# Splitting the statistics and the read of g into halves of a group in a fused hypergraph block

## The reference

```
def hypergraph_conv(x, adj, W, b):
    H = (adj != 0);  w = adj.reshape(N, -1)[:, :C]
    xw = einsum('ncd,hd->nch', x, W)
    Dn = 1 / einsum('nce,ne->nc', H, w)      # 0 where the sum is not positive
    Be = 1 / H.sum(axis=1)
    m = Be[:, :, None] * einsum('nce,nch->neh', H, xw)
    return Dn[:, :, None] * einsum('nce,neh->nch', H, m) + b

h = relu(hypergraph_conv(x, adj, W1, b1))    # 256 -> 512 features
h = layer_norm(h, gamma, beta)
y = hypergraph_conv(h, adj, W2, b2) + x      # 512 -> 256 features
out = layernorm(x + y)                       # over the 256 features, no gain or shift
```

## Time and profile before

| | us |
|---|---|
| median of 3 runs (302.49 to 303.74) | 303.43 |
| the profiled execution | 302.48 |
| its span, from first to last instruction | 300.6 |
| TensorE matmuls busy | 285.8 (95%) |
| TensorE weight loads busy | 253.5 (84%) |
| ScalarE busy | 212.6 (71%) |
| VectorE busy | 208.4 (69%) |
| GpSimd busy | 126.6 (42%) |

### The profile page before, as it was taken

One profiled execution on the slowest core, in us unless ns is written; L12 is line 12 of the kernel. 1 busy time (PEld: TensorE's weight loads), 2 busy tenths in 40 slices (PEclk: granted clock), 3 DMA queues, 4 the chain that ended last, 5 costly groups with the idle time before them and its releaser, 6 DMA issues.

```text
span 300.6 us, 5790 instructions
## 1 busy us (share of the span) xinstructions
PE 285.8 (95%) x1866; PEld 253.5 (84%) x1866; DVE 208.4 (69%) x587; ACT 212.6 (71%) x621; POOL 126.6 (42%) x163
## 2 busy tenths in 40 slices
PE   7799999999999999999999999999999999999991
PEld 6689879798988979898897989889797988979790
DVE  2788496785758577585858758594866859385784
ACT  3497869688585968858596886859688685755514
POOL 2236162707245270714527171543617063362462
PEclk9999999999999999999999999999999999999998
DMA  7920500505133050603315060311405210020104
GB/s 223 293 67 20 159 0 17 177 1 164 31 88 107 20 173 2 182 13 91 101 28 167 2 193 0 113 47 20 142 1 157 73 50 22 0 72 1 70 2 140
DMA packets 33510, 24.27 MB, mean 81 GB/s; under 512 B 7932, under 2 KB 33224, under 8 KB 33480
## 3 DMA queue, kind: packets, MB, share of 16 engines
q1 hardware_dynamic: 33376, 23.86, 26.7%
q10 hardware_dynamic: 104, 0.04, 0.1%
HBM read 13.80 MB, written 8.39 MB: 74 GB/s over the span
## 4 chain that ended last, share of the span: by engine, by line
PE 40%; DVE 16%; POOL 16%; ACT 15%; issue 11%; DVEq 0%; POOLq 0%
PE bank_v L259 10%; PE bank_v L308 10%; POOL rstd L844 7%; ACT ht_sb L429 5%; DVE bn_sb L684 5%; PE bank_s L238 5%; POOL rstd L866 5%; DVE g_sb L641 5%; PE bank_v L274 4%; ACT scratch L488 4%; ACT r_sb L466 3%; POOL r_hi L859 3%; PE bank_g L301 2%; PE bank_g L284 2%; PE bank_g L291 2%
## 5 line engine op out<-in xcount | busy, mean ns | idle before, releaser
L284 PE MATMUL bank_g<-w_hi,r_hi 128*128 128x258 f32 x256 | 65.5, 288 | 0.0
L286 PE MATMUL bank_g<-w_lo,r_hi 128*128 128x256 f32 x256 | 63.8, 282 | 0.0
L866 POOL TENSOR_TENSOR rstd<-var,half_power 128x4 f32<-128x4 f32 (+1 forms) x17 | 17.7, 1043 | 105.8 <-DVE var L698 105.8
L650 DVE TENSOR_TENSOR r_lo<-r_sb,r_hi 128x512 fp32r<-128x512 f32 x64 | 42.7, 688 | 27.5 <-POOL r_hi L859 27.5
L859 POOL TENSOR_SCALAR r_hi<-r_sb 128x512 fp32r<-128x512 f32 x64 | 40.8, 638 | 35.0 <-ACT r_sb L466 35.0
L466 ACT ACTIVATE r_sb<-bank_v,vec 128x512 f32<-128x512 f32 x64 | 44.1, 689 | 11.8 <-PE bank_v L274 11.2
L274 PE MATMUL bank_v<-u_hi,w_hi 128*128 128x512 f32 x128 | 50.7, 396 | 0.4 <-DVE u_lo L610 0.4
L274 PE MATMUL bank_v<-u_hi,w_lo 128*128 128x512 f32 x128 | 50.8, 397 | 0.0
L274 PE MATMUL bank_v<-u_lo,w_hi 128*128 128x512 f32 x128 | 50.6, 396 | 0.0
L284 PEld LDWEIGHTS bank_g<-w_hi,r_hi 128*128 128x128 f32 x256 | 48.3, 189 | 1.4
L286 PEld LDWEIGHTS bank_g<-w_lo,r_hi 128*128 128x128 f32 x256 | 48.2, 188 | 1.2
(11 more groups left out here) (98 smaller groups left out, 464.8 us busy)
## 6 DMA issues: line engine op xcount, KB each, us to landing
x_sb<-in_x_dram SPq DMA_DIRECT2D x16, 512.0 KB, 3.9
out_dram<-z_sb SPq DMA_DIRECT2D x15, 512.0 KB, 3.2
adj_sb<-in_adj_dram SPq DMA_DIRECT2D x16, 256.0 KB, 3.8
w_raw<-in_L_gnn_W_dram SPq DMA_DIRECT2D x2, 512.0 KB, 5.5
out_dram<-z_sb SPq DMA_DIRECT2D x2, 256.0 KB, 2.5
turned_h<-h_sb SPq DMA_TRANSPOSE x13, 2.4
b_half<-in_L_gnn_b_dram SPq DMA_DIRECT2D x1, 128.0 KB, 9.0
edge_rows<-in_adj_dram ACTq DMA_DIRECT2D x1, 32.0 KB, 3.3
```

What stands on the lines that cost most here:

```text
L284: pe.matmul(bank_g[:, n, 0:W2COLS], r_hi[:, i % 2, k, graph(n)], w2_hi[:, k], start=(k == 0), stop=False)
L286: pe.matmul(bank_g[:, n, 0:DOUT], r_hi[:, i % 2, k, graph(n)], w2_lo[:, k], start=False, stop=False, skip_group_check=True)
L650: nc.vector.tensor_tensor(r_lo[:, i % 2, k], r_sb[:, k], r_hi[:, i % 2, k].bitcast(F32), ALU.subtract).then_inc(r_lo_ready, 1)
```

## The change

make_var1, inverse_std1 and read_g, which took the four graphs of a group at once, now take two at a time in every group (before, in the last group alone). For this g_made and q_summed are raised after every second graph. xb is made in two instructions, one behind each first power on GpSimd, for the next group. In VectorE's order the first half's statistics and read stand ahead of make_var2, which is that of the group before.

```diff
             def make_g(i, n):
                 if n == PER - 1:
-                    pe.wait_ge(q_summed, i + 1)
+                    pe.wait_ge(q_summed, 2 * i + 2)
...
-                if n == PER - 1 or (i == LAST and n == PER // 2 - 1):
+                if n % 2:
                     mm.then_inc(g_made, 1)
...
             def sum_q(i):
                 act.wait_ge(q_turned, i + 1)
                 if i:
-                    act.wait_ge(var1_ready, i)
+                    act.wait_ge(var1_ready, i * 2)
                 for n in range(PER):
                     ins = nc.scalar.activation(scratch[:, n], turned_q[:, graph(n)], ACT.Copy,
                                                accum_out=sum_sq[:, n:n + 1])
-                    if i == LAST and n == PER // 2 - 1:
-                        ins.then_inc(last_q_half, 1)
-                ins.then_inc(q_summed, 1)
+                    if n % 2:
+                        ins.then_inc(q_summed, 1)
...
-            def make_var1(i, half=None):
-                part, done = graphs(half), i + (half or 0)
+            def make_var1(i, half):
+                part, done = graphs(half), i * 2 + half
...
-            def read_g(i, half=None):
+            def read_g(i, half):
...
-                dve.wait_ge(rstd1_ready, i + (half or 0) + 1)
-                for h in range(2) if half is None else (half,):
-                    for n in each(h):
-                        ins = nc.vector.scalar_tensor_tensor(out=g_sb[:, n], in0=bank_g[:, n, 0:DOUT],
...
+                dve.wait_ge(rstd1_ready, i * 2 + half + 1)
+                for n in each(half):
+                    ins = nc.vector.scalar_tensor_tensor(out=g_sb[:, n], in0=bank_g[:, n, 0:DOUT],
...
                     take_stats2(i - 1, 0)
                     take_stats2(i - 1, 1)
+                make_var1(i, 0)
+                read_g(i, 0)
+                if i:
                     make_var2(i - 1)
                     if i + 4 < G:
                         make_h(i + 4)
                 split_r(i + 1, 0)
-                make_var1(i)
+                make_var1(i, 1)
                 if i == 0:
                     make_b(3)
+                read_g(i, 1)
                 split_r(i + 1, 1)
                 add_pair(i + 1, 0)
-                read_g(i)
...
-            def inverse_std1(i, half=None):
+            def inverse_std1(i, half):
                 part = graphs(half)
-                pool.wait_ge(var1_ready, i + (half or 0) + 1)
+                pool.wait_ge(var1_ready, i * 2 + half + 1)
...
-            def add_b2(i):
+            def add_b2(i, half):
+                part, n = graphs(half), len(each(half))
...
-                nc.gpsimd.tensor_tensor(xb_sb[:, i % 2], x_sb[:, i % 3],
-                                        b2_half[:, :].unsqueeze(1).to_broadcast([P, PER, DOUT]),
-                                        ALU.add).then_inc(xb_ready, 1)
+                nc.gpsimd.tensor_tensor(xb_sb[:, i % 2, part], x_sb[:, i % 3, part],
+                                        b2_half[:, :].unsqueeze(1).to_broadcast([P, n, DOUT]),
+                                        ALU.add).then_inc(xb_ready, 1 if half is not None else 2)
...
                 if i + 3 < G:
                     copy_w(i + 3)
+                inverse_std1(i, 0)
+                add_b2(i + 1, 0)
+                split_r(i + 1, 0)
                 if i:
                     inverse_std2(i - 1)
-                split_r(i + 1, 0)
                 split_r(i + 1, 1)
-                inverse_std1(i)
+                inverse_std1(i, 1)
+                add_b2(i + 1, 1)
                 split_r(i + 1, 2)
-                if i + 1 < LAST:
-                    add_b2(i + 1)
                 split_r(i + 1, 3)
-            pool.wait_ge(q_ready, G)
-            add_b2(LAST)
```

More of the change, by code:

```diff
@@ L141, in hypergraph_block @@
         out_ready, last_out_ready = sem("out_ready"), [sem("last_out_low"), sem("last_out_high")]
[L142 removed]
+        last_shift2_ready = sem("last_shift2_ready")
         def graph(n):
@@ L297, in turn_q @@
                 pe.wait_ge(q_ready, i + 1)
-                pe.wait_ge(q_summed, i)
+                pe.wait_ge(q_summed, i * 2)
                 pe.wait_ge(g_ready, i * 2)
@@ L401, in _ @@
             pe.wait_ge(consts_ready, 5)
-            pe.wait_ge(xb_ready, G)
+            pe.wait_ge(xb_ready, G * 2)
             for n in range(PER):
@@ L408, in _ @@
                 else:
-                    pe.wait_ge(q_summed, G)
+                    pe.wait_ge(q_summed, G * 2)
                 pe.matmul(last_z[n], ident_2[:, :], xb_sb[:, 1, n], start=True, stop=False)
@@ L620, in make_var1 @@
                                         ALU.mult).then_inc(stat1_step, 1)
[L621 to L624, removed]
+                dve.wait_ge(q_summed, done + 1)
                 dve.wait_ge(stat1_step, done * 3 + 2)
@@ L648, in split_r @@
                 if i >= 2:
-                    dve.wait_ge(g_made, i - 1)
+                    dve.wait_ge(g_made, (i - 1) * 2)
                 nc.vector.tensor_tensor(r_lo[:, i % 2, k], r_sb[:, k], r_hi[:, i % 2, k].bitcast(F32),
@@ L672, in make_z @@
                         dve.wait_ge(stored[i % 2], landed(i - 2, 2))
-                    dve.wait_ge(xb_ready, i + 1)
+                    dve.wait_ge(xb_ready, (i + 1) * 2)
                 dve.wait_ge(y_made, i * 2 + (half + 1))
@@ L839, in copy_w @@
                                       edge_cols[:, j * PER:(j + 1) * PER]).then_inc(wcol_ready, 1)
-            def inverse_std1(i, half=None):
+            def inverse_std1(i, half):
                 part = graphs(half)
-                pool.wait_ge(var1_ready, i + (half or 0) + 1)
+                pool.wait_ge(var1_ready, i * 2 + half + 1)
                 nc.gpsimd.tensor_tensor(rstd1[:, part], stat1[:, 3, part], half_power[:, part],
                                         ALU.pow).then_inc(rstd1_ready, 1)
-            def add_b2(i):
+            def add_b2(i, half):
+                part, n = graphs(half), len(each(half))
                 pool.wait_ge(x_in[i % 3], landed(i, 3))
-                if i >= 2:
+                if i >= 2 and half != 1:
                     pool.wait_ge(z_ready, (i - 1) * 2)
-                nc.gpsimd.tensor_tensor(xb_sb[:, i % 2], x_sb[:, i % 3],
-                                        b2_half[:, :].unsqueeze(1).to_broadcast([P, PER, DOUT]),
-                                        ALU.add).then_inc(xb_ready, 1)
+                nc.gpsimd.tensor_tensor(xb_sb[:, i % 2, part], x_sb[:, i % 3, part],
+                                        b2_half[:, :].unsqueeze(1).to_broadcast([P, n, DOUT]),
+                                        ALU.add).then_inc(xb_ready, 1 if half is not None else 2)
             def split_r(i, k):
@@ L857, in split_r @@
                 if i >= 2:
-                    pool.wait_ge(g_made, i - 1)
+                    pool.wait_ge(g_made, (i - 1) * 2)
                 nc.gpsimd.tensor_scalar(r_hi[:, i % 2, k], r_sb[:, k], 1.0, 1.0, ALU.mult,
@@ L901, in _ @@
             copy_w(2)
-            add_b2(0)
+            add_b2(0, None)
             for i in range(LAST):
```

8 lines of the change are left out of this document (4 added, 4 removed).

## The result

The changed kernel takes 327.27 us (median of 4 runs, 326.02 to 327.38), the kernel before on the same chip 303.02 (four runs, 302.49 to 303.74). The ratio is 1.0789, with a 95% interval of 1.0752 to 1.0827. The profiled execution of the changed kernel took 326.02 us with a span of 324.1, where before it was 302.48 and 300.6: 23.5 us more in the span, where the prediction had 17.7.

What follows compares the result with a forecast made beforehand. TensorE bounds the kernel, busy 17.11 of 17.38 us a group. Group 0's 1.5, 12 x 1.33 = 16.0, 0 and 0.2 sum to 17.7 us on 302.48: 320.2, forecast 321 by the median; likeliest 316 to 327, low end widened to 313.

Steps and rivals of the forecast that it cites:

- Steps 1, 2 and 4: First statistic to GpSimd's power 0.91 us, half power 0.70, half of xb 1.24; second power starts 2.48 us later.
- Step 3: VectorE waits 0.9 us for the half power; bn_aggr starts at 138.60 instead of 136.24, var2 reaches GpSimd 0.74 us after.
- Step 5: GpSimd's second power takes 1.27 us, 0.15 more than now, with r_lo and part of h_sb beside it.
- D: How much later the shift comes to ScalarE: 2.48 + 0.15 = 2.63 us; a group loses D minus 1.30.
- The slack: From relu 3 to y's second half: 0.78 us plus 0.35 of ScalarE's idle time, together 1.13 us.
- That gives 0.17 us back: On TensorE u follows y's late second half directly, in 0.98 us, instead of 1.15 us waiting for z.
- The rest is covered: Second half's power and read of g have 1.4 us of cover before y; later xb, h_sb and store cost nothing.
- Groups 12 to 14: Group 12 loses 1.33 us like groups 1 to 11, group 13 nothing, group 14 0.2 us.
- Group 0: make_b(3) stands behind var1(0, 1), so ScalarE's htb(3) starts at 39.3 instead of 37.48; the loss is 1.5 us.
- y waiting for the second read of g: Rival: y's second half waits for that read rather than relu 3; 6 us more, 327; chance 0.07.
- The faster rival: D stays under 1.30, no relu is late, y starts 0.31 us earlier in 14 groups: 298.3 us; chance 0.06.
- The clock rival: TensorE's clock falls in the new gaps, matmuls behind them at half speed in twelve groups: 36 us more, 357; chance 0.02.

Runs made afterwards that it cites:

- e4: The changed kernel with both halves of normalise moved behind the last square on ScalarE: 306.56 us, 1.0132 of the kernel before.
- e5: The changed kernel with r_lo(1) and the first pair back ahead of the second half's read of g on VectorE: 323.29 us, 1.0671 of the kernel before.
- e2: The changed kernel with GpSimd's second power directly behind the first, both halves of xb behind the second half's power: 330.55 us, 1.0928 of the kernel before.
- e10: The changed kernel with make_b(3) directly behind the first read of g in group 0 on VectorE: 325.69 us, 1.0766 of the kernel before.
- e9: The changed kernel with the edits of e4, e5 and e10 together: 297.26 us, 0.9817 of the kernel before.
- e6: The changed kernel with the edits of e4 and e5 together: 300.02 us, 0.9891 of the kernel before.
- e3: The changed kernel with make_var2 and make_h ahead of the first half's statistics on VectorE, GpSimd's order kept: 336.13 us, 1.1106 of the kernel before.
- e1: The changed kernel with make_var2 and make_h ahead of the first half's statistics, and GpSimd's second power first again: 317.10 us, 1.0484 of the kernel before.
- e8: The kernel before the change with xb made in two half-size instructions, one behind the other, at its old place: 302.58 us, 0.9994.

## Why the prediction was nearly right, and where it was off

The direction and the main mechanism were right: var2 behind a new wait, the shift late, the relus behind normalise, make_v and y behind the relus. e4 takes the relus out from behind the shift and brings 20.7 us back; e5, with the second cause out of the way, shows 1.29 us a group for 1.33. The whole was too small by 5.8 us in the span. The median, 327.27, lies 0.3 us above the likeliest range (316 to 327), and that it came so near its end is luck: the high end was built from a slower half of xb and a slower power, and neither is what took the time in the twelve steady groups.

- **Steps 1, 2 and 4, the half power and half of xb.** From the first statistic to the power 0.90 us (146.10 to 147.00), where 0.91 was forecast. Half power 0.71 for 0.70, half of xb 1.30 for 1.24. VectorE's wait 0.91 for 0.9.
- **Step 3, the handover of var2.** It was left at 0.74 us and measured 1.13 (148.61 to 149.74), so the tie went to VectorE, and GpSimd waited 0.17 us for it. `mean` took 0.58 us and not 0.17. It ends at 149.60, r_hi beside it at 149.57, and where GpSimd idles (e2) it takes 0.17. So the term in step 3 was mis-sized: its duration was taken from a place where GpSimd was idle. By the Trainium skill (SBUF — State Buffer, section "SBUF: two separate sides"), of a contending VectorE and a GpSimd instruction the one that starts first holds the shared way into SBUF to its end; `mean` ending with r_hi agrees.
- **Step 5, the second power.** Forecast 1.27 us; 1.12 in group 6, the same as before the change, since var2 was late enough for r_lo to start only at 149.90, behind the power's start at 149.74. In group 13 there is no h_sb, r_lo starts first, and the same power takes 1.43 us. The timeline of VectorE in group 13 of the change:

```profile
281.20 0.57 DVE L692 TENSOR_SCALAR mean<-mv_sb 128x4 f32<-128x4 f32 x1
...
281.79 0.69 DVE L645 TENSOR_TENSOR r_lo<-r_sb,r_hi 128x512 fp32r<-128x512 f32 x1
```

And GpSimd at the same place:

```profile
281.92 1.43 POOL L865 TENSOR_TENSOR rstd<-var,half_power 128x4 f32<-128x4 f32 x1 [0.17 <-DVE var L693]
```

- **D.** 2.72 where 2.63 was forecast. The second power starts 7.85 us into the group (149.74 - 141.89) instead of 5.13, 2.72 later and not 2.48, which is step 3's 0.24; step 5's 0.15 didn't come. Two errors that nearly cancel, so that D came out right is no proof of the steps.
- **The slack.** y's second half was to come 1.50 us later and came 1.41 later, but with D at 2.72 the slack was 2.72 - 1.41 = 1.31 and not 1.13. From relu 1 to relu 3 ScalarE gained 0.60 us (155.63 - 152.17 = 3.46 where it was 143.47 - 139.41 = 4.06), for the 0.35 counted. So part of the time behind relu 1 that was taken for work was given back, and no run here shows why. The handover from relu 3 to y is 0.14 us, for the 0.05 taken from g_sb to y. Again two errors that go against each other.
- **"That gives 0.17 us back" is the step that failed.** u was to follow y's second half directly, in 0.98 us. It came after 1.33, since it waits for z; in e5, where it doesn't, it comes after 0.94. By the periods of the change and e5 this wait costs 18.99 - 18.67 = 0.32 us a group, 3.8 over 12 groups, the largest part of the 5.8 that were missing. The prediction moved the second read of g later and asked only whether y would wait for it; it didn't ask what stands behind it on VectorE. r_lo(1) and pair_sb stand there, then z. In the change they take 0.90 and 1.09 us, beside GpSimd's half of xb and r_hi, and 0.69 each in e5, where they run ahead of the read.
- **The sentence "The rest is covered"** was therefore wrong in its scope. The second read of g itself was on time; z behind it was not.
- **Groups 12 to 14.** Forecast: group 12 as the others, 0 in 13, 0.2 in 14. Measured: 1.93, 0.76 and 0.77. None of the three has an h_sb, so r_lo starts ahead of the second power, which takes 1.43 or 1.44 us; the 0.32 us over the 1.12 of the other groups are what group 12 loses beyond their 1.61. In groups 13 and 14 the small `mean` (0.57) is there too. In group 13 the first half's statistics also wait 0.26 us for g, until 278.28, which the forecast had nowhere, and there the forecast left no slack at all, so that a longer path had to show.
- **Group 0.** Forecast 1.5, measured 1.96. htb(3) starts at 39.60 for the 39.3 forecast. e10 shows that this delay hides two others of nearly the same size.
- **The rivals.** y waiting for the second read of g (327) is not what happened in the steady groups, though the time comes out the same: the 14 waits listed under g_sb, 3.4 us, are those for relu 2. In group 6 the second read ends at 155.20 and y's second half starts at 156.44, a cover of 1.24 us for the 1.4 forecast. The faster rival needed D under 1.30; e9 has it in another way, the late shift made harmless, and its 297.26 us are near what that rival gave (298.3). In the change's profiled execution the granted clock is 1.00 in group 6 and behind the gap of group 0. The clock rival did not come true in the steady groups; for group 0 see below.

By terms: 17.7 + 12 x (1.61 - 1.33) + 0.32 more in group 12 + 0.76 and 0.57 in groups 13 and 14 + 0.46 in group 0 + 0.39 in the rest = 23.6, the 23.5 of the spans within the rounding.

## What to carry to other kernels

When an instruction is moved later on an engine, walk down its queue to every instruction behind it that a bounding engine waits for, and compute that engine's slack at each; here z, and with it u, hung on the moved read of g as the relus hung on the moved shift, and the smaller delay lay mostly under the larger. Take a small instruction's duration from a place where GpSimd is as busy as it will be beside it. A change that is right in itself can lose because a consumer stands behind the wrong producer: what made an early g pay was to put normalise, which nothing waits for soon, behind the relus, and the second read of g behind the work that z doesn't need to wait for.

## What the runs showed of the hardware that was not expected

- Instructions of VectorE and GpSimd take longer where they overlap, and how much goes by which of them starts first. GpSimd's power of four columns takes 1.02 us beside an idle VectorE, 1.12 with h_sb beside it, whether r_lo starts behind it (the change, group 6) or much later (e2), and 1.43 when r_lo is running as it starts; the power of two columns 0.71 alone and 1.08 beside r_lo in e9. A pair of r_hi takes 2.08 us in the change and 1.19 in e9. On VectorE a `mean` of 128x4, with one SBUF input, goes from 0.17 to 0.58 us, r_lo from 0.69 to 0.90, pair_sb from 0.69 to 1.09 and to 1.76. By the Trainium skill (GPSIMD Engine Reference, section 1) VectorE instructions with two SBUF inputs, or in a 2-port mode, contend. r_lo agrees; for `mean`, with one input, the trace fits the second condition, but no run here shows its mode.
- The granted clock can fall behind the gap of 2.4 us that TensorE has in group 0, and need not. The windows view of the change there (columns as in the earlier trace rows):

```profile
39.00:42.00 3.00, 0.59 (x4) 0.41 (x3) 2.32 (x8) 2.37 (x6) 2.42 (x3) 1.00 0.00 0
42.00:45.00 3.00, 2.86 (x18) 2.25 (x17) 2.53 (x4) 1.83 (x5) 1.10 (x3) 1.00 0.00 0
```

  And of e6, with the same gap from 39 to 42:

```profile
39.00:42.00 3.00, 0.60 (x4) 0.43 (x3) 2.44 (x8) 2.39 (x7) 2.65 (x3) 1.00 0.00 0
42.00:45.00 3.00, 2.86 (x10) 2.10 (x9) 0.80 (x2) 1.67 (x4) 1.19 (x3) 0.60 0.00 0
```

  In the second the clock is at its lower level (1.2 GHz) for most of the next stretch, and group 0 takes 15.48 us instead of 14.07. The same fall is in the profiles of e3 (0.51) and e4 (0.73). The four executions of e6 fit it: 299.97 to 300.06 us with a mean granted clock of 0.989 to 0.991, and 298.55 with 0.994. Of the change itself, the execution of 326.02 us has a mean granted clock of 0.994, and those of 327.21 to 327.38 have 0.989 or 0.990. 0.0045 of 325 us are 1.5 us of full clock missed, about the 1.3 us between them. So the median of the change probably holds this fall, and part of what e10 and e9 gain beyond their profiled differences would be that it's gone. That isn't shown: no trace of the change itself has it. Two things speak for care. The kernel before ran in 302.48 to 302.49 us with mean granted clocks from 0.993 to 0.998, and single executions also differ ahead of group 0: the first g matmul starts at 24.97 us in the profiles of e1 and e5 and at 25.31 in that of e8, but at 24.05 in that of the change. In e9 TensorE is busy for 1.83 of the 3.00 us from 39 to 42, the clock stays at 1.00, and its four runs lie within 0.1 us.
